# A graph network on one core: ScalarE fetches one tile of each 32 groups in the relation passes, SyncE scatters 39 columns of records beside the attention

## The reference, cut to what matters

```python
# 1 attention over edges, softmax per dst node
a = einsum('ehd,ehd->eh', q[src], k[dst]) / sqrt(32)
ex = exp(a - segment_max(a, dst)[dst])
agg = segment_sum(v[src] * (ex / segment_sum(ex, dst)[dst])[:, :, None], dst)
# 2 relations, both directions of each edge
msg = xw[et_all, src_all]            # xw = x @ weight[r]
out = sum_r(segment_sum(msg, r * n + dst_all) / degree) + x @ self_weight
# 3 GINE: MLP(segment_sum(x[dst] + edge_attr_16 @ W_edge + b, src)), batch norm
# 4 edge convolution: relu(segment_sum(x[src] @ W + b + edge_attr_6 @ We + be, dst))
```

## Time and profile before

| | us |
|---|---|
| median of 3 runs | 15097.61 (15036.07, 15097.61, 15100.59) |
| the profiled execution | 15048.15 |
| its span, first to last instruction | 15046.4 |
| GpSimd busy | 11040.0 (73%) |
| VectorE busy | 9777.3 (65%) |
| TensorE busy | 8799.8 (58%) |
| ScalarE busy | 2786.0 (19%) |

### The profile page before, as it was taken

One profiled execution on the slowest core, in us unless ns is written; L12 is line 12 of the kernel. 1 busy time (PEld: TensorE's weight loads), 2 busy tenths in 40 slices (PEclk: granted clock), 3 DMA queues, 4 the chain that ended last, 5 costly groups with the idle time before them and its releaser, 6 DMA issues. The chain is left out here.

```text
span 15046.4 us, 271687 instructions
## 1 busy us (share of the span) xinstructions
PE 8799.8 (58%) x56575; PEld 6746.2 (45%) x56575; DVE 9777.3 (65%) x34050; ACT 2786.0 (19%) x7303; POOL 11040.0 (73%) x11322
## 2 busy tenths in 40 slices
PE   6766667777777777555555555555344444544444
PEld 2212226666666666244444444444333333433334
DVE  8877777888888788866666677777533333433333
ACT  0011114444444443421111111111100000200000
POOL 4777767777777777777777777777677776577776
PEclk8876669999999999755555555555555555655555
DMA  2011122222222222422222222222222222322223
GB/s 85 7 42 50 53 64 70 69 69 69 70 68 70 69 69 67 155 82 59 59 59 59 58 63 63 63 63 63 68 64 63 63 64 69 112 63 61 62 62 84
DMA packets 741583, 1005.24 MB, mean 67 GB/s; under 512 B 272537, under 2 KB 535954, under 8 KB 739826
## 3 DMA queue, kind: packets, MB, share of 16 engines
q0 software_dynamic: 387968, 670.55, 17.1%
q1 hardware_dynamic: 331986, 313.98, 6.8%
q10 hardware_dynamic: 20000, 3.33, 0.1%
HBM read 801.67 MB, written 185.28 MB: 66 GB/s over the span
## 5 line engine op out<-in xcount | busy, mean ns | idle before, releaser
L1827 DVE TENSOR_TENSOR acc<-banks,acc 128x128 f32 x3328 | 969.6, 291 | 2599.9 <-PE banks L1785 2232.1
L657 POOL DMA_INDIRECT rec_dst<-stage_dst_sort,row_dst_sort x1563 | 1565.5, 1002 | 645.7 <-issue 474.7
L783 POOL DMA_INDIRECT far_att<-table_qv,recs_att x1664 | 1628.2, 978 | 521.4 <-issue 506.8
L783 POOL DMA_INDIRECT far_sum_dst<-table_h,recs_sum_dst x1613 | 1560.6, 968 | 580.4 <-issue 491.7
L783 POOL DMA_INDIRECT far_sum_src<-table_h,recs_sum_src x1613 | 1557.1, 965 | 563.6 <-issue 491.8
L783 POOL DMA_INDIRECT far_rel_src<-table_xw,recs_rel_src x1638 | 1571.6, 959 | 508.1 <-issue 493.5
L783 POOL DMA_INDIRECT far_rel_dst<-table_xw,recs_rel_dst x1638 | 1557.2, 951 | 510.1 <-issue 494.2
L1605 DVE TENSOR_TENSOR acc<-banks,acc 128x128 f32 x3328 | 969.7, 291 | 1115.4 <-PE banks L1531 996.3
L919 POOL DMA_INDIRECT rec_src<-moved_att,row_src x1248 | 1243.4, 996 | 397.1 <-issue 380.1
L1785 PE MATMUL banks<-far_sum_src,hot_sum_src 128*128 128x128 f32 x3226 | 827.7, 438 | 1200.9 <-DVE hot_sum_src L1818 851.8
L1785 PE MATMUL banks<-far_sum_dst,hot_sum_dst 128*128 128x128 f32 x3226 | 824.2, 436 | 1152.1 <-DVE hot_sum_dst L1818 930.1
(11 more groups left out here) (332 smaller groups left out, 21490.4 us busy)
## 6 DMA issues: line engine op xcount, KB each, us to landing
lone_sync_rel_dst<-table_xw SPq DMA_DIRECT2D x3328, 0.5 KB
lone_sync_rel_src<-table_xw SPq DMA_DIRECT2D x3328, 0.5 KB
lone_sync_sum_src<-table_h SPq DMA_DIRECT2D x3328, 0.5 KB
lone_sync_sum_dst<-table_h SPq DMA_DIRECT2D x3328, 0.5 KB
lone_scalar_sum_src<-table_h ACTq DMA_DIRECT2D x3200, 0.5 KB
lone_scalar_sum_dst<-table_h ACTq DMA_DIRECT2D x3200, 0.5 KB
table_xw<-xw_rel_tables SPq DMA_DIRECT2D x98, 512.0 KB, 2.8
far_att<-table_qv,recs_att POOLq DMA_INDIRECT x1664
```

Source lines behind the costliest of these rows:

```text
L657: e.indirect_dma_start(out=flat_dst, out_offset=bass.IndirectOffsetOnAxis(ap=row["dst"][:, c + i:c + i + 1], axis=0), in_=stage["dst"][:, ...
L783: e.indirect_dma_start(out=self.far[:, g % RING, t, :], out_offset=None, in_=table, in_offset=bass.IndirectOffsetOnAxis(ap=index, axis=0)) ...
L1827: e.tensor_tensor(acc[:, bass.ds(at[t], 1), :], sums[g0 % 4][:, t:t + 1, :], acc[:, bass.ds(at[t], 1), :], ALU.add).then_inc(k.s_sum, 1)
```

## The change

Two edits. In the relation passes ScalarE now fetches one tile of each 32 groups (13 a pass) row by row, four rows behind each copy of `hot_t`, and GpSimd gathers 13 fewer. `Stream` gets a spacing (`every`) and a first one (`start`) for each fetching engine; the numbers read lie in `row_src`, free by then. In attention 39 of 1248 columns (the last column of each block c with c % 8 in 0, 3, 6) are scattered by SyncE instead of GpSimd, one DMA a record from `raw_src` to `rec_src` in DRAM, 48 records a block. For it `row_src` is first copied to DRAM (`row_list`), and a column's 128 places are read back into one partition.

```diff
@@ -30,7 +30,9 @@
 LONE = 16
 LONES = GROUPS // LONE
-assert GROUPS % LONE == 0
+LONE_REL = 32
+assert GROUPS % LONE_REL == 0
 NT = GROUPS * GT
 BLOCKS = NT // BT
 CH = 32
@@ -44,6 +46,10 @@
 MOVE = 12
 MOVES = BLOCKS
+SOLE = [c for c in range(MOVES) if c % 8 in (0, 3, 6)]
+SOLE_ROWS = len(SOLE) * P // BLOCKS
+assert SOLE_ROWS * BLOCKS == len(SOLE) * P and SOLE_ROWS % 8 == 0
 LATER = ET - MOVES * MOVE
 assert LATER > 0
@@ -752,8 +760,10 @@
 class Stream:
-    def __init__(self, k, s, recs, far=None, lone=None, ids=None):
+    def __init__(self, k, s, recs, far=None, lone=None, ids=None, every=None, start=None):
+        self.every, self.start = every or {}, start or {}
         self.k, self.rec, self.recs, self.far = k, k.rec[s], recs, far
         self.lone, self.ids = lone or {}, ids
         self.rec_base, self.ring_base, self.lone_base = k.rec_base, list(k.ring_base), {n: list(b) for n, b in k.lone_base.items()}
@@ -768,10 +778,10 @@
     def fetcher(self, g, t):
-        if g % LONE != LONE - 1:
+        name = {GT - 1: "sync", GT - 2: "scalar"}.get(t)
+        if name not in self.lone or (g + 1) % self.every[name] or g // self.every[name] < self.start.get(name, 0):
             return None
-        name = {GT - 1: "sync", GT - 2: "scalar"}.get(t)
-        return name if name in self.lone and (name == "sync" or g >= LONE) else None
+        return name
     def tiles(self, g):
@@ -788,7 +798,7 @@
     def far_rows(self, g, t):
         name = self.fetcher(g, t)
-        return self.lone[name][:, g // LONE % 2, :] if name else self.far[:, g % RING, t, :]
+        return self.lone[name][:, g // self.every[name] % 2, :] if name else self.far[:, g % RING, t, :]
     def fetched(self, e, g):
@@ -833,11 +841,22 @@
         if self.far is not None:
             self.k.ring_base = [self.gathered(GROUPS - RING + r)[1] for r in range(RING)]
         for name in self.lone:
-            for b in range(2):
-                self.k.lone_base[name][b] += 16 * P * self.turns(name, LONES - 2 + (LONES - 2 + b) % 2)
+            last = GROUPS // self.every[name] - 1
+            for s in (last - 1, last):
+                self.k.lone_base[name][s % 2] += 16 * P * self.turns(name, s)
 assert BLOCKS % NREC == 0 and GROUPS % RING == 0
+def columns_of(c):
+    return MOVE - (c in SOLE)
+def placed(c):
+    return 16 * sum(columns_of(i) for i in range(c % NREC, c + 1, NREC))
 def steps(leads):
@@ -886,11 +906,33 @@
         s_hot, s_chill, s_widen, s_weight, s_fade, s_flat, s_key, s_spread, s_top_row, s_turn, s_product, s_top, s_sum, \
             s_score, s_below, s_reduce, s_mix, s_away, s_clear, s_keys = (k.sem(f"s_a_{n}") for n in names)
-        def placed(c):
-            return 16 * MOVE * (c // NREC + 1)
         def sync(e):
+            numbered = {}
+            def number(s):
+                t = SOLE[s] * MOVE + MOVE - 1
+                k.ids_count["sync"] += 16
+                with k.nc.allow_non_contiguous_dma(reason="one number of each record"):
+                    e.dma_start(ids[0:1, s % 2, :], k.row_list[:, t:t + 1].bitcast(I32).rearrange("p c -> c p")).then_inc(k.s_ids["sync"], 16)
+                return k.ids_count["sync"]
+            def single_rows(c):
+                for r in range(c * SOLE_ROWS, (c + 1) * SOLE_ROWS, 8):
+                    s, first = divmod(r, P)
+                    t = SOLE[s] * MOVE + MOVE - 1
+                    if first == 0:
+                        e.wait_ge(k.s_ids["sync"], numbered[s])
+                        if s + 1 < len(SOLE):
+                            numbered[s + 1] = number(s + 1)
+                    to = e.bass.values_load_multi_w_load_instructions(
+                        ids[0:1, s % 2, first:first + 8], engines=[e.engine], min_val=0, max_val=P * NT - 1,
+                        skip_runtime_bounds_check_because="the ranks are those of the records' own places")[1]
+                    for i in range(8):
+                        p = first + i
+                        e.dma_start(flat_src[bass.ds(to[i], 1), :], k.raw_src[p:p + 1, t, :]).then_inc(k.s_lone["sync"][0], 16)
             for c in range(BLOCKS):
                 if c >= NREC:
                     e.wait_ge(s_sum, 2 * GT * (c - NREC + 1) * RG)
@@ -900,8 +942,17 @@
                 b = c % NREC
                 if c >= NREC:
                     e.wait_ge(k.s_placed[b], placed(c - NREC))
-                e.dma_start(moved[:, b, :, :], k.raw_src[:, c * MOVE:(c + 1) * MOVE, :]).then_inc(k.s_moved[b], 16)
+                m = columns_of(c)
+                e.dma_start(moved[:, b, 0:m, :], k.raw_src[:, c * MOVE:c * MOVE + m, :]).then_inc(k.s_moved[b], 16)
+                if c == 0:
+                    k.ids_count["scalar"] += 16
+                    e.dma_start(k.row_list, k.row_src[:, :].bitcast(F32)).then_inc(k.s_ids["scalar"], 16)
+                    e.wait_ge(k.s_ids["scalar"], k.ids_count["scalar"])
+                    numbered[0] = number(0)
+                single_rows(c)
             e.wait_ge(s_keys, 16)
+            e.wait_ge(k.s_lone["sync"][0], single0 + 16 * P * len(SOLE))
         def gpsimd(e):
             for g in range(GROUPS):
@@ -914,7 +965,7 @@
                 b = c % NREC
                 if first == 0:
                     e.wait_ge(k.s_moved[b], 16 * (c // NREC + 1))
-                for i in range(first, first + MOVE // RG):
+                for i in range(first, min(first + MOVE // RG, columns_of(c))):
                     t = c * MOVE + i
                     e.indirect_dma_start(out=flat_src, out_offset=bass.IndirectOffsetOnAxis(ap=k.row_src[:, t:t + 1], axis=0),
                                          in_=moved[:, b, i, :], in_offset=None).then_inc(k.s_placed[b], 16)
@@ -1436,8 +1488,11 @@
     with ExitStack() as ctx:
         sb = scratch(k, ctx, f"rel_{side}")
-        lone, ids = {"sync": sb("lone_sync", [P, 2, F])}, {"sync": sb("ids_sync", [1, 2, P], I32)}
-        st = Stream(k, side, sb("recs", [P, NREC, BT, COLS[side]]), sb("far", [P, RING, GT, F]), lone, ids)
+        lone = {n: sb(f"lone_{n}", [P, 2, F]) for n in ("sync", "scalar")}
+        ids = {n: k.row_src[0:1, i * 2 * P:(i + 1) * 2 * P].rearrange("a (s p) -> a s p", p=P) for i, n in enumerate(("sync", "scalar"))}
+        st = Stream(k, side, sb("recs", [P, NREC, BT, COLS[side]]), sb("far", [P, RING, GT, F]), lone, ids,
+                    {"sync": LONE, "scalar": LONE_REL})
         win, acc, more, n_more, n_att = k.win[side], k.acc, k.more[side], MORE[side], ATTRS[side]
         hot = sb("hot", [P, 4, GT, P], BF16)
         kind = sb("kind", [P, 4, GT, R])
@@ -1507,6 +1562,19 @@
                 e.wait_ge(k.s_rest, b0 + c + 1)
                 e.copy(parts(c, 1), rest[:, :, :]).then_inc(k.s_mid, 1)
+            def single_rows(g):
+                s, i = divmod(g, LONE_REL)
+                share = P // LONE_REL
+                if i == 0:
+                    if s >= 2:
+                        e.wait_ge(k.s_product, p0 + (s - 1) * LONE_REL)
+                    e.wait_ge(k.s_ids["scalar"], numbered[s])
+                    if s + 1 < GROUPS // LONE_REL:
+                        numbered[s + 1] = st.number_rows(e, "scalar", s + 1, IDX8)
+                st.fetch_rows(e, "scalar", s, k.table_xw, i * share, share)
+            numbered = {0: st.number_rows(e, "scalar", 0, IDX8)}
             high(0)
             middle(0)
             high(1)
@@ -1519,6 +1587,7 @@
                 if g >= 4:
                     e.wait_ge(k.s_look, q0 + g - 3)
                 e.copy(hot_t[:, g % 4, :, :], turned[g % 2]).then_inc(k.s_flat, 1)
+                single_rows(g)
         def tensor(e):
             for g3, g2, g0 in steps((3, 2, 0)):
@@ -1681,7 +1750,9 @@
     with ExitStack() as ctx:
         sb = scratch(k, ctx, f"sum_{side}")
         lone, ids = {n: sb(f"lone_{n}", [P, 2, F]) for n in ("sync", "scalar")}, {n: sb(f"ids_{n}", [1, 2, P], I32) for n in ("sync", "scalar")}
-        st = Stream(k, side, sb("recs", [P, NREC, BT, COLS[side]]), sb("far", [P, RING, GT, F]), lone, ids)
+        st = Stream(k, side, sb("recs", [P, NREC, BT, COLS[side]]), sb("far", [P, RING, GT, F]), lone, ids,
+                    {"sync": LONE, "scalar": LONE}, {"scalar": 1})
         HOT = 6
         hot = sb("hot", [P, HOT, GT, P])
         win, acc, p0 = k.win[side], k.acc, k.passes * GROUPS
```

More of the change, by code:

```diff
@@ L116, in build_program @@
         k.raw_src = dram("raw_src", [P, ET, CS])
+        k.row_list = dram("row_list", [P, ET])
         k.conv = dram("conv_rows", [P, W, F])
@@ L135, in build_program @@
         k.lone_base = {"sync": [0, 0], "scalar": [0, 0]}
+        k.ids_count = {"sync": 0, "scalar": 0}
         k.s_store = [k.sem(f"s_store{i}") for i in range(4)]
@@ L798, in fetched @@
             if name:
-                s = g // LONE
+                s = g // self.every[name]
                 e.wait_ge(self.k.s_lone[name][s % 2], self.lone_base[name][s % 2] + 16 * P * self.turns(name, s))
     def turns(self, name, s):
```

(19 more changed lines are left out.)

## The result

| | before | after |
|---|---|---|
| median, us | 15096.12 (4 runs) | 16701.74 (4 runs, 16632.92 to 16742.3) |
| ratio to before | | 1.1067, 95% interval 1.1039 to 1.1095 |
| the profiled execution, us | 15048.15 | 16632.92, span 16631.2 |

The account below looks back on a forecast made before the run. GpSimd's instruction count was taken to bound attention and relation passes. Savings of 83.4 us less 6 at the start gave 77: 14971 from the profiled run, 15021 from the median; the middle, 14996, was rounded to 14995, range 14945 to 15085.

Parts of the forecast that it names:

- GpSimd bounds the passes, and an instruction less shortens them: Attention and relation passes: GpSimd's instruction count sets their length; fewer instructions save 50.7, 16.3 and 16.4 us.
- the sum: Whole kernel: 83.4 us saved on GpSimd less 6 us at attention's start, 77 us gained.
- What it adds on SyncE in attention: SyncE in attention: 4992 record DMAs at 0.508 us each, 25.2 us a block against GpSimd's 35.7.
- the far end: SyncE in attention: highest cost allowed for a record, 0.71 us, making a block 34.9 us.
- Both ends fit: SyncE in attention: blocks of 25.2 us and of 34.9 us both stay within GpSimd's 35.7 us.
- a delay of 25 us in it reaches nobody: SyncE in attention: the next block's record load runs about two blocks ahead, so 25 us of delay harms nothing.
- Rival 3: Attention: SyncE bounds it, from 0.73 us a record; at 0.80 the kernel takes 15316 us or more; chance 0.08.
- The start of attention: GpSimd at attention's start: waits 4.6 us for block 1's records, 14 us at 0.71 a row; 6 taken.
- ScalarE in the relation passes: Relation passes: four rows, 2.03 us, fill ScalarE's 3.9 us wait, which falls to about 1.5; cost 0.
- Rival 1: Relation passes: collisions with VectorE lengthen gathers to 1.270 us, losing 44 us, 15037 to 15065; chance 0.10.
- rival 2: Attention: record DMAs make scatters and gathers 1% longer, losing 37 us, 15008 to 15058; chance 0.14.
- The two pairs of runs: Whole kernel: runs before lay near 15036 and 15048 or 15098 and 15101, giving 14971 or 15021 after.
- The two rules: Skill's rules: two-input VectorE instructions contend with GpSimd reading SBUF; transfers under 512 B are read-modify-write.

Follow-up runs that it names:

- experiment 2: Changed kernel, but SyncE loads a column's 128 records into on-chip memory in one DMA and scatters each from there: ratio 0.9954, median 15013.95 us.
- experiment 3: Changed kernel, but each SyncE DMA moves 19 of a record's 21 numbers, DRAM to DRAM in one piece: 15966.89 us, one run.
- experiment 6: Kernel of experiment 2 with 52 columns by SyncE instead of 39, 64 records a block: ratio 0.9945.
- experiment 9: Changed kernel, but SyncE's record DMAs write to a fixed DRAM address, without register; records don't reach their place: 15075.06 us, one run.
- experiment 7: Kernel of experiment 2, with ScalarE fetching a tile of each 16 groups in the relation passes instead of each 32: ratio 0.9941.
- experiment 4: Changed kernel with 26 columns by SyncE instead of 39, 32 records a block, still in seven pieces: ratio 0.9964.

## Why the prediction was wrong

- **GpSimd bounds the passes, and an instruction less shortens them.** Right for the kernel before, in the relation passes (15.9 us of forecast 16.3; 23.0 of 16.4, where gathers also came out 4 ns shorter, 1625 x 0.004 = 6.5 us), and in attention once SyncE keeps up (experiment 2). The closeness of 15.9 to 16.3 is partly luck: with the same 1625 gathers the pass `dst` lasts 2034.4 (experiment 3) to 2046.1 us (experiment 6). With this step mended, experiment 2 is 69.6 us faster than the kernel before (15083.56 - 15013.95), where the sum had 77.
- **"What it adds on SyncE in attention": this step failed.** It took 0.508 us a record from a fetch of DRAM to on-chip memory and called 0.71 the far end, by the issue of a 128-partition tile; "Both ends fit." A record took (52.0 - 0.85) / 48 = 1.07 us: 0.72 for the DMA instead of 0.23, with 1.03 instead of 0.78 us for each register load. Both neighbours had one end on chip, and a DMA with both ends in DRAM stood in no row. The bound was not one: nothing excluded that such a DMA was slower than the slowest of another kind. Experiments 2, 3 and 9 show that this is the property that counts (227 ns, then 576 in one piece; 648 at a fixed address), the cut into pieces second. So SyncE's block was 52.0 us where "25.2 us, at the far end 34.9 us" stood, and "a delay of 25 us in it reaches nobody" fell with it: the load two blocks ahead covers a delay once, not one of 16 us in every block.
- **Rival 3 had the mechanism, the place and the point from which it decides**, 0.73 us a record. With 1.07 its sum gives 104 x (48 x 1.07 + 0.8) = 5425 us against 5398 measured. Its chance, 0.08, came from the false far end. The order had shown `7x3` and the unseen kind; with a threshold 1.4 times the taken value and a price of hundreds of microseconds, the chance should have been several times that, and the range open above. That is a judgement; no run shows it.
- **The start of attention.** Right within 1 us: 4.6 us worked out, 3.7 measured in experiment 2, where the wait stands alone, and 3.9 in experiment 7. In the changed kernel itself the 48 records took 49.8 us instead of 24.4, and the load of block 1 went at 2308.24 us.
- **ScalarE in the relation passes.** Right that nothing is late; the forecast that its wait would fall to 1.5 us was not: 1302.3 / 392 = 3.3 us, since the profile counts the issuing of DMAs as idle. Less 1.63 us for the rows and 0.48 for the register load it is about 1.2: the forecast had the room about right and the figure of the profile wrong. A queue's room must be read from its timeline.
- **Collisions and contention (rivals 1 and 2).** Rival 1 did not come in the relation passes: 951 and 955 ns. (The lower end of its range, 15037, doesn't follow: 15048 - 33 is 15015.) Its mechanism came elsewhere, in the scatters of attention: 11 ns each in experiment 2 and 20 in experiment 4, 13 and 24 us. The median doesn't move, and in the changed kernel, where scatters took 983 ns, it all but vanishes, so these traces give rival 2 no support. The sum pass `src` shows how much such collisions move without any edit there: its gathers take 965 ns in the kernel before and 989 in experiment 4, the pass 2047.9 and 2085.5 us. A difference of some 20 us in one stage of one profile is therefore not yet an effect of the edit.
- **The two pairs of runs.** The forecast built on 15036 to 15048 and 15098 to 15101 as two places. In three later sets the kernel before ran from 15013 to 15111 us with values all through, and each set has a median of its own. The two places were a chance of few runs.
- **The two rules.** The first, on engines contending, didn't decide the result; where it shows in the traces is said just above. The size of the records under 512 B did not slow SyncE's queue: the same 84 bytes to the same places cost 227 ns in experiment 2.

## What to carry to other kernels

Before moving work to a queue that has room, price the new instruction by one with the same two ends (on chip or DRAM) and the same cut; where no row shows it, set its break-even against the period of the engine it must keep up with, and give a break-even only 1.4 times the guess a real chance. If many small copies go from DRAM to DRAM on SyncE, load them on chip in one DMA and send them from there: here this turned 1.107 into 0.995. (Issued on ScalarE's queue, such copies were not tried.) A queue's loads for the next stage stand behind whatever is put in it, so the sum of a block's issues has to stay below the block. And compare medians beside means: a mean that moves while the median stands points at a few long instructions, and so at their timing.

## What the runs showed of the hardware that was not expected

- Issue on SyncE of one record, median: on chip to DRAM 227 ns; DRAM to DRAM 576 (one piece), 717 (seven), 734 (ten), 497 (sixteen); seven pieces at a fixed address 648. These differ in size too (84, 76, 84, 80, 64 and 84 bytes). A plain load of 128 partitions behind the records in seven pieces rose too, from 320 to 430 ns. The Trainium skill (DMA: Bandwidth & Descriptors, Why a DMA increments its semaphore by 16 and not by 1) says that a DMA of fewer than 16 engines has its remaining increments written by the sequencer itself. Sixteen pieces being cheaper than seven would fit that, ten costing more than one doesn't follow from it, and no run here shows how many engines a record's DMA used. Why both ends in DRAM take 350 ns more in one piece stays open; it was not tried whether ScalarE's queue shows the same.
- A register load of eight numbers took 1032 ns behind DRAM-to-DRAM records in one, seven or ten pieces, 525 behind those in sixteen, and 782 behind records sent from on chip.
- GpSimd's indirect DMAs have two lengths. In attention before, in experiments 2 and 4 and after, all that take over 1.15 us start beside a 128x512 f32 `tensor_tensor` of VectorE (before: 128 of the 812 that do, none of the 2100 others).
